# A gated two-state delta-rule block: the second gate's beta moves into the second inverse on GpSimd, and the query products move from VectorE to GpSimd

## The reference

```python
kn = k_t / jnp.maximum(jnp.linalg.norm(k_t, axis=-1, keepdims=True), 1e-12)
pred = jnp.einsum('bhji,bhj->bhi', S, kn)
r = jnp.clip(v_t - pred, -CLIP, CLIP)
S = a_t[..., None] * S
kp = jnp.einsum('bhd,bhde->bhe', kn, S)
S = S + b_t[..., None, None] * kn[..., None] * (v_t - kp)[..., None, :]
o = jnp.einsum('bhji,bhj->bhi', S, q_t)
R = aR_t[..., None] * R
kpR = jnp.einsum('bhd,bhde->bhe', kn, R)
R = R + g_t[..., None, None] * kn[..., None] * (r - kpR)[..., None, :]
o = o + jnp.einsum('bhji,bhj->bhi', R, q_t)
```

## Time and profile before

| what | before |
|---|---|
| median of 3 runs (lowest to highest) | 3480.25 us (3474.77 to 3484.2) |
| the profiled execution: time, span | 3481.59 us, 3479.8 us |
| PE, PEld, DVE, ACT, POOL busy, share of the span | 84%, 74%, 76%, 56%, 35% |
| TensorE's granted clock, mean | 0.889 of full speed |
| `attention`, 62 to 2575 us: DVE busy | 2227.43 of 2513 us |
| one chunk in the middle, N to N (1284.40 to 1363.13 us) | 78.73 us |

### The profile page before, as it was taken

How to read it: one execution, slowest core, us unless ns; L and a number is a source line. 1 busy time by engine, 2 the same in 40 slices (tenths; PEclk the granted TensorE clock), 3 DMA queues, 4 the chain that set the end, 5 groups by cost and what they waited for, 6 DMA issues and landing times. The chain is left out here.

```text
span 3479.8 us, 135741 instructions
## 1 busy us (share of the span) xinstructions
PE 2906.5 (84%) x56922; PEld 2571.7 (74%) x56922; DVE 2644.2 (76%) x6931; ACT 1948.5 (56%) x5132; POOL 1229.9 (35%) x1001
## 2 busy tenths in 40 slices
PE   4888888888888888889988888888855998889980
PEld 4888887878888887878888887888744776667760
DVE  3899988999998988998898989898952444444444
ACT  3555665665555655665555665565523555655550
POOL 3122322222222323222222322222222666666664
PEclk8998888899999889988898889898877999999995
DMA  3211111111111111111111111111147777767766
GB/s 122 78 54 41 35 38 41 38 38 42 38 35 36 40 35 40 42 38 41 39 35 35 41 35 39 43 35 36 44 154 242 116 115 113 114 108 115 115 107 210
DMA packets 193480, 240.15 MB, mean 69 GB/s; under 512 B 26738, under 2 KB 171251, under 8 KB 192115
## 3 DMA queue, kind: packets, MB, share of 16 engines
q1 hardware_dynamic: 132896, 151.22, 14.4%
q0 software_dynamic: 58368, 75.80, 13.7%
q10 hardware_dynamic: 1618, 4.46, 0.3%
HBM read 96.17 MB, written 135.20 MB: 66 GB/s over the span
## 5 line engine op out<-in xcount | busy, mean ns | idle before, releaser
L391 POOL DMA_INDIRECT table<-xrow,place_i x256 | 280.4, 1095 | 764.0 <-DVE BR L866 237.8
L1475 PE MATMUL bank<-w,route 128*128 x2560 | 370.8, 288 | 35.7 <-issue 12.2
L1105 POOL COPY inv_r<-N 32x512 f32<-32x512 f32 x128 | 136.4, 1065 | 736.5 <-DVE N L842 732.5
L1475 PEld LDWEIGHTS bank<-w,route 128*128 128x128 f32 x2560 | 311.9, 192 | 104.2 <-issue 101.2
L457 DVE TENSOR_TENSOR tri<-tri,step 128x58 f32<-128x58 f32 (+13 forms) x896 | 305.5, 341 | 30.8
L456 DVE TENSOR_TENSOR step<-tri 128x58 f32<-128x58 f32 (+13 forms) x896 | 301.7, 337 | 26.4
L1490 PE MATMUL bank<-w,seen 128*128 x640 | 215.0, 418 | 52.5 <-DVE y L1563 10.2
L1551 DVE COPY to_row<-shared 128x1 int32<-128x1 int32 x228 | 35.1, 154 | 269.1 <-DMA acc<-sh_h,to_row 43.3
L1082 POOL COPY T<-L_s 32x512 f32<-32x512 f32 x64 | 38.7, 605 | 359.5 <-DVE L_s L778 358.2
L1490 PEld LDWEIGHTS bank<-w,seen 128*128 128x128 f32 x640 | 95.8, 189 | 89.2 <-issue 83.8
L589 PE MATMUL bank<-B,kT_r 64*64 64x64 f32 x2048 | 110.4, 300 | 61.4 <-DVE S L883 61.4
(11 more groups left out here) (306 smaller groups left out, 8864.7 us busy)
## 6 DMA issues: line engine op xcount, KB each, us to landing
table<-blank SPq DMA_DIRECT2D x320, 129.0 KB
shared<-table SPq DMA_DIRECT2D x228, 129.0 KB
w<-in_wpack_dram SPq DMA_DIRECT2D x16, 1540.0 KB
xrow<-table SPq DMA_DIRECT2D x92, 129.0 KB
sum<-acc SPq DMA_DIRECT2D x16, 512.0 KB
acc<-blank SPq DMA_DIRECT2D x33, 128.0 KB, 2.6
x_rows<-y SPq DMA_DIRECT2D x64, 64.0 KB
x_res<-in_x_dram SPq DMA_DIRECT2D x64, 64.0 KB
```

The lines of the kernel that those rows point to most:

```text
L391: nc.gpsimd.indirect_dma_start(out=table, out_offset=bass.IndirectOffsetOnAxis(ap=t.place8_i[:, k:k + 1], axis=0), in_=row[:, :], in_offse ...
L1105: ins = nc.gpsimd.tensor_copy(t.inv[1][r, :, Q * (q % 2):Q * (q % 2) + Q], t.N[r, 16:32, :])
L1475: mm = nc.tensor.matmul(ps[:, begin:begin + n], t.xT_slot[i % 3][:, P * kt:P * kt + P], weights(i, 257 * kt + begin, n), start=(kt == 0), ...
```

## The change

The factor beta of the second gate leaves VectorE (line 866 is dropped, the subtraction of line 865 raises `BR_ready` itself). Since W is the product of the second inverse with that correction, the factor is multiplied onto `inv[1]` instead: GpSimd's four copies of line 1105 become four products of N with beta, and two more products on GpSimd scale the off-diagonal blocks in place once ScalarE has put them there. Between them GpSimd makes the first two coefficient halves; the last two follow. TensorE's own wait for X1 before W goes, because GpSimd now has it. The two query products and `dec_end` leave VectorE's list, where they stood between the sums into S and R, and stand in GpSimd's between the scatters 6 and 7, behind `dec_ready`, the copied queries (`q1`) and `O_begun`. Scatter 7 and the diagonal copies come behind them.

```diff
--- before.py
+++ after.py
@@ -161,7 +161,7 @@
              "dve_link", "act_link", "ln_var_ready", "ln_guess_ready", "xhat_ready", "x2_made", "res_ready",
              "keys_squared", "norm_ready", "bg_exp_ready", "beta_ready", "key_ready",
              "coef_ready", "act_diag", "pool_diag", "restart_ready", "queries_made",
-             "N_ready", "T_ready", "inv_s_ready", "inv_r_ready", "B_ready", "BR_ready", "O_begun", "O_done",
+             "N_ready", "T_ready", "inv_s_ready", "inv_r_begun", "inv_r_ready", "B_ready", "BR_ready", "O_begun", "O_done",
              "scan_done", "log_ready", "dec_ready", "plus_made", "states_ready", "pool_link", "xf_ready",
              "x2_stored", "sh_stored", "sh_ready", "sel_ready", "rec_ready", "zero_stored",
              "late_loaded", "zeros_ready", "tiny_ready",
@@ -491,9 +491,9 @@
     return nc.scalar.activation(t.bgz[:].rearrange("p g u -> p (g u)"), ps[:, 0:32], ACT.Exp, scale=-1.0)
 
 
-def row_coefficients(nc, t, beta):
-
-    for g, h in STREAMS:
+def row_coefficients(nc, t, beta, streams):
+
+    for g, h in streams:
         half = slice(8 * h, 8 * h + 8)
         nc.gpsimd.tensor_tensor(t.L[g][:, half, :], bc(beta[:, g, half], C), over(t.neg_strict[:], 8),
                                 ALU.mult).then_inc(t.sem["coef_ready"], 1)
@@ -720,7 +720,6 @@
                 ps = begin(n, "SD")
                 wait_emptied(pe, t, o, n, "SG")
                 shared_down(nc, t, ps).then_inc(t.sem["front_mm"], 1)
-                wait_emptied(pe, t, o, n, "X1")
                 pe.wait_ge(t.sem["inv_r_ready"], n + 1)
                 pe.wait_ge(t.sem["BR_ready"], 2 * n + 2)
                 crossed(n, "W", [(of(t.inv[1]), of(t.BR))])
@@ -862,8 +861,7 @@
                     wait_emptied(dve, t, o, n, f"PR{h}")
                     link(nc.vector.tensor_scalar(r, r, -1.0, 1.0, ALU.max, ALU.min))
                     wait_emptied(dve, t, o, n, "KR1")
-                    link(nc.vector.tensor_tensor(r, r, rest, ALU.subtract))
-                    nc.vector.tensor_tensor(r, r, bc(t.beta[n % 2][:, 1, h:16:2], C), ALU.mult).then_inc(t.sem["BR_ready"], 1)
+                    nc.vector.tensor_tensor(r, r, rest, ALU.subtract).then_inc(t.sem["BR_ready"], 1)
                 if route:
                     dve.wait_ge(t.sem["sel_ready"], o.base("sel_ready", n + 1))
                     route_weights(nc, t, link, t.xrow[n % 2])
@@ -882,11 +880,6 @@
                     ps = mm(n, f"SU{h}")
                     nc.vector.tensor_tensor(t.S[:, half[h], :], blk(ps[:, :]), t.S[:, half[h], :],
                                             ALU.add).then_inc(t.sem["dve_emptied"], 1)
-                if front:
-                    wait_emptied(dve, t, o, n, "q1")
-                    nc.vector.tensor_tensor(t.pq[:, 1, :, :], t.q[:], t.dec[:, 0, :, :], ALU.mult)
-                    nc.vector.tensor_tensor(t.rqplus[:], t.q[:], t.dec[:, 1, :, :], ALU.mult)
-                    nc.vector.tensor_copy(t.dec_end[(n + 1) % 2][:], t.dec[:, :, :, C - 1]).then_inc(t.sem["queries_made"], 1)
                 for h in range(2):
                     ps = mm(n, f"RU{h}")
                     nc.vector.tensor_tensor(t.R[:, half[h], :], blk(ps[:, :]), t.R[:, half[h], :],
@@ -1102,22 +1095,41 @@
                 pool.wait_ge(t.sem["N_ready"], n + 1)
                 for q in range(4):
                     r = slice(Q * q, Q * q + Q)
-                    ins = nc.gpsimd.tensor_copy(t.inv[1][r, :, Q * (q % 2):Q * (q % 2) + Q], t.N[r, 16:32, :])
+                    ins = nc.gpsimd.tensor_tensor(t.inv[1][r, :, Q * (q % 2):Q * (q % 2) + Q], t.N[r, 16:32, :],
+                                                  bc(t.beta[n % 2][r, 1, :], Q), ALU.mult)
+                ins.then_inc(t.sem["inv_r_begun"], 1)
+                pool.wait_ge(t.sem["inv_r_begun"], n + 1)
+                if front:
+                    wait_done(pool, t, o, n, "Z1")
+                    pool.wait_ge(t.sem["beta_ready"], n + 1)
+                    row_coefficients(nc, t, t.beta[(n + 1) % 2], STREAMS[0:2])
+                    pool.wait_ge(t.sem["coef_ready"], o.base("coef_ready", n) + 2)
+                wait_emptied(pool, t, o, n, "X1")
+                for j in range(2):
+                    r = slice(C * j, C * j + Q)
+                    ins = nc.gpsimd.tensor_tensor(t.inv[1][r, :, Q:2 * Q], t.inv[1][r, :, Q:2 * Q],
+                                                  bc(t.beta[n % 2][r, 1, :], Q), ALU.mult)
                 ins.then_inc(t.sem["inv_r_ready"], 1)
                 pool.wait_ge(t.sem["inv_r_ready"], n + 1)
                 if front:
-                    wait_done(pool, t, o, n, "Z1")
-                    pool.wait_ge(t.sem["beta_ready"], n + 1)
-                    row_coefficients(nc, t, t.beta[(n + 1) % 2])
+                    row_coefficients(nc, t, t.beta[(n + 1) % 2], STREAMS[2:4])
                 if n >= 2:
                     pool.wait_ge(t.sem["BR_ready"], 2 * n + 1)
                     scatter_row(nc, t, d.table, t.xrow[(n - 1) % 2], 5)
                     pool.wait_ge(t.sem["BR_ready"], 2 * n + 2)
                     scatter_row(nc, t, d.table, t.xrow[(n - 1) % 2], 6)
+                if front:
+                    pool.wait_ge(t.sem["dec_ready"], 2 * n + 2)
+                    wait_emptied(pool, t, o, n, "q1")
                     pool.wait_ge(t.sem["O_begun"], n + 1)
+                    nc.gpsimd.tensor_tensor(t.pq[:, 1, :, :], t.q[:], t.dec[:, 0, :, :], ALU.mult)
+                    nc.gpsimd.tensor_tensor(t.rqplus[:], t.q[:], t.dec[:, 1, :, :], ALU.mult)
+                    nc.gpsimd.tensor_copy(t.dec_end[(n + 1) % 2][:], t.dec[:, :, :, C - 1]).then_inc(t.sem["queries_made"], 1)
+                if n >= 2:
                     scatter_row(nc, t, d.table, t.xrow[(n - 1) % 2], 7)
                     wait_scattered(pool, t, n - 1)
                 if front:
+                    pool.wait_ge(t.sem["queries_made"], o.base("queries_made", n) + 1)
                     diagonal(n)
 
 
@@ -1169,7 +1181,7 @@
                                     t.k[:].rearrange("p u n -> p (u n)"), ALU.mult).then_inc(t.sem["keys_squared"], 1)
             pool.wait_ge(t.sem["beta_ready"], 1)
             pool.wait_ge(t.sem["late_loaded"], 16 * len(late))
-            row_coefficients(nc, t, t.beta[0])
+            row_coefficients(nc, t, t.beta[0], STREAMS)
             pool.wait_ge(t.sem["key_ready"], 1)
             for g in range(2):
                 pool.wait_ge(t.sem["dec_ready"], g + 1)
```

## The result

The changed kernel takes 3630.7 us (median of 4 runs, 3624.89 to 3639.37), beside 3481.61 us for the kernel before on the same chip: 1.0433 of it, 95% interval 1.0407 to 1.046. The forecast was 3621 us, between 3535 and 3680. The profiled execution's span is 3623.1 us (before 3479.8), its mean granted clock 0.866 (before 0.889).

What follows compares the result with a forecast made beforehand. VectorE's list bounds the long stretch, TensorE/ScalarE's chain the first, and k to S, RU, triangles and L_s the middle. Per chunk 4.24 + 0.1 + 0.2 = 4.54 us, 141 over 31 chunks, gave 3621 us; range 3535 to 3680.

Steps and rivals of the forecast that it cites:

- VectorE takes turns with GpSimd for SBUF: Behind k: GpSimd's two query products get in between c, kplus and pq, each holding VectorE 2.12 us.
- the 0.83 us: First stage: delay of VectorE's small `dec_end` copy, queued behind k, by a waiting GpSimd product of 1.04 us.
- 2.12 us per product, 4.24 for two: Between k and S: each GpSimd query product of 2.33 us holds VectorE for its duration less 0.21 us.
- The scan's lower bound of 2.6: Lower bound for both query products, 1.3 us each, scaled from a scan that paid 0.34 us beside a GpSimd copy.
- The 0.21 us: Part of a GpSimd instruction's duration that does not delay VectorE, taken from the first stage: 1.04 us product, 0.83 us delay.
- 0.1 us for GpSimd's copy of `dec_end`: Behind kplus or pq: GpSimd's `dec_end` copy holds VectorE between 0 and 0.2 us, taken as 0.1.
- 0.2 us for the clock: Triangles and output projection: TensorE's lower clock after a longer idle before RU costs 0.2 us per chunk, between 0 and 1.7.
- The shed 3.8 us count for nothing: Beta and query products leaving VectorE save 3.8 us per chunk, all in front of waits for others.
- The longer GpSimd list hides: Between N and BR: ten GpSimd products, 10.4 against 6.5 us, cost 0, at worst about 0.5 us per chunk.
- VectorE keeps the operands: Rival, chance 0.12: c, kplus and pq go through as one block, GpSimd works behind them; 3480 us.
- one product alone gets onto the path: Rival, chance 0.10: first query product gets in, second stays out until S; 2.2 us per chunk, 3549 us.
- the shed work counts in full: Rival "Faster", chance 0.05: VectorE's shed 3.8 us per chunk count, 0 to 118 us, down to 3362 us.

Runs made afterwards that it cites:

- the run with S ahead of pq: Against the changed kernel: GpSimd's query products wait for S, scatter 7 goes first, and VectorE adds S before making pq; 3465.98 us, ratio 0.9951.
- Half products: Kernel before with only query products and the `dec_end` copy moved to GpSimd, the products covering 8 of 16 heads; 3539.55 us, ratio 1.016.
- the run without products: Changed kernel with GpSimd's two query products left out in the chunks, the copy of `dec_end` kept; 3466.16 us, ratio 0.9959.
- beta alone: Changed kernel with the query products back on VectorE, so only beta's move to GpSimd remains; 3472.72 us, ratio 0.9966.
- S ahead of pq without them: Kernel before, nothing moved to GpSimd, with S added ahead of pq on VectorE; 3470.26 us, ratio 0.998.
- products behind the copy: Run with products behind S and S ahead of pq, but GpSimd's products wait for the small copy behind pq instead of S; 3439.07 us, ratio 0.9882.
- products behind S: Changed kernel, same work per engine, but scatter 7 goes first and GpSimd's query products wait until S is added; 3461.86 us, ratio 0.9952.

## Why the prediction was right

- *VectorE takes turns with GpSimd for SBUF, and a waiting GpSimd instruction goes before a queued VectorE one.* Right, and the place of each turn as forecast (c, kplus, pq). Moving the release alone undoes it (3461.86 us), and in the run with S ahead of pq a waiting product took its turn ahead of a copy queued behind pq, which then took 2345 ns in the mean of 31 chunks. One reading was too narrow: the prediction sets the 0.83 us beside a rule for VectorE instructions with two SBUF inputs, but that was a copy with one, and so is the one of 2345 ns. What matches the rule for two inputs are the scans there, and c and kplus now.
- *2.12 us per product, 4.24 for two.* Measured 4.22 from k to S. The scan's lower bound of 2.6 was too low. Half products cost 2.12 for two, where the same rule gave 1.92: the part that is hidden is nearer 0.1 than 0.21 us there. The 0.21 us came from a single meeting of two instructions, so it is partly luck that whole products agree within 0.02 us per chunk; I would trust the rule to about 0.1 us a turn.
- *0.1 us for GpSimd's copy of `dec_end`.* Too much; k to S is 6.90 us with that copy alone (the run without products), and in the changed kernel what c, kplus and pq took longer (4.24 us) leaves nothing of the 4.22 us for it. It was held up itself, with 2.01 us in the mean.
- *0.2 us for the clock.* Too little. S to L_s lost 0.29 us and L_s to N 0.26, while the first stretch gained 0.13: 0.42 in all. TensorE spends 24.4 us of a chunk at 1.2 GHz in place of 18.2, beside an idle of some 6.8 us before RU (209.9 us in 31 chunks). The waits that grew are those for TensorE, in front of L_s from 16.4 to 24.7 us and of pqT from 11.3 to 16.4, as the step had it; that the clock alone lengthened them no run isolates. With these two misses the chunk is 4.66 us longer against 4.54 forecast, which is 4 of the 10 us between 3621 and 3631. The profiled execution itself took 3624.89 us, 143 more than the one before; the other 6 us are the spread of the executions around it (3624.89 to 3639.37).
- *The shed 3.8 us count for nothing.* Nearly: 14 us of 118, by the run without the products. I had not foreseen the gain of 11 us with beta alone; its cause is open, TensorE's clock being the only difference that I found.
- *The longer GpSimd list hides.* Right for the end of it (N to k 23.17 against 23.30), and close to its limit: I had a wait of 3.3 us left before the norms in the chunk shown, and 2.65 was there, 1.97 in the mean. The scans cost 0.7 us, as estimated, and the routing between them and BR 2.0 us, within the 1 to 2.5 estimated.
- *The rivals.* That VectorE keeps the operands, or that one product alone gets onto the path, is refuted by c, kplus and pq in every run with the products beside them; that the shed work counts in full, by the run without them.

## What to carry to other kernels

Ask of work that is moved to GpSimd which VectorE instructions stand in the list when it is released: one that reads SBUF cost a VectorE instruction with two SBUF operands, or a small copy in SBUF, nearly its full length here, even if that instruction was queued directly behind another. Release it where VectorE works from PSUM, by a signal from the last SBUF instruction of VectorE, and not by the event that happens to make its data free. And what VectorE sheds is worth next to nothing in front of a wait. The products released behind S gave 0.5%, and S ahead of pq without them 0.2%; the two moves with the release behind pq's copy gave 1.2%, 41 us.

## What the runs showed of the hardware

- A GpSimd product of 2.33 us delayed VectorE by 2.11 us, one of half the length by 1.06, and a copy of 0.18 us queued behind pq grew to 2.35 us; two GpSimd fills of 1.43 us, which read nothing, did not delay it (k to S 6.87 us against 6.90).
- GpSimd and VectorE alternated: c took at most 4.33 us and kplus at most 4.44 in the 31 chunks of the changed kernel, so two products never passed one waiting VectorE instruction.
- An indirect DMA issue on GpSimd that met c took up to 3.10 us in the kernel before, where undisturbed ones took 0.98, and ended 0.86 us behind c, but kplus behind c kept 2.28 us: this GpSimd instruction waited for VectorE and did not hold it up in turn.
- Beside a wait of TensorE for S of 6.8 us in the mean stood 24.4 us per chunk at the lower clock (after), beside 2.0 us 18.2 (before), and beside 0.7 us 15.3 (products behind the copy), where RU took 2.1 us in most chunks instead of some 3.5. The wait does not set the clock by itself: beside 3.9 us stood 18.6 (half products), and beside 1.9 us 16.0 (products behind S).
